# Expert tiles of a cross-attention and mixture-of-experts kernel: gathered rows turned by a transposing DMA instead of by TensorE

## What is computed

```python
x = x + xattn(layernorm(x), ctx)        # x: (4, 1024, 1024), ctx: (4, 1024, 512)
x = x + ffn(layernorm(x))               # 4096 tokens in all
# xattn: q, k = ctx @ Wq.T + bq, ctx @ Wk.T + bk ; attention = softmax(q @ k.T)
#        returns einsum('bln,bmn->blm', layernorm(x), attention)
# ffn, a mixture of 32 experts, 4 of them for each token (H = 1024, I = 512):
logits = x @ gate_w.T + gate_b
top, idx = top_k(logits, 4); weight = softmax(top)
gate = min(xt @ w_gate[e] + b_gate[e], 7); up = clip(xt @ w_up[e] + b_up[e], -7, 7)
act = (up + 1) * gate * sigmoid(1.702 * gate)
y += weight * (act @ w_down[e] + b_down[e])
```

## Time and profile before

| | us |
|---|---|
| median of 3 runs (lowest, highest) | 3435.58 (3431.8, 3443.01) |
| span of the profiled execution | 3448.7 |
| PE busy | 3170.0 (92%) |
| DVE busy | 1738.2 (50%) |
| ACT busy | 1266.2 (37%) |
| POOL busy | 582.6 (17%) |

### The profile page before, as it was taken

How to read it: one execution, slowest core, us unless ns; L and a number is a source line. 1 busy time by engine, 2 the same in 40 slices (tenths; PEclk the granted TensorE clock), 3 DMA queues, 4 the chain that set the end, 5 groups by cost and what they waited for, 6 DMA issues and landing times.

```text
span 3448.7 us, 46558 instructions
## 1 busy us (share of the span) xinstructions
PE 3170.0 (92%) x15456; PEld 1607.2 (47%) x15457; DVE 1738.2 (50%) x2850; ACT 1266.2 (37%) x1299; POOL 582.6 (17%) x502
## 2 busy tenths in 40 slices
PE   6899899987999999999999999999999999999997
PEld 3455555553444444444444444444444444444443
DVE  4576677673444444545544544454444444454432
ACT  4444444333332433334333434343333433332321
POOL 0033323331111111111111111111111111111111
PEclk8899999988999999999999999999999999999999
DMA  3223222354543554645545546564555445454422
GB/s 142 79 105 117 100 94 104 121 168 153 141 140 98 146 140 140 195 136 169 158 134 141 180 132 180 160 182 123 139 175 161 139 141 146 136 164 126 110 61 55
DMA packets 210440, 468.05 MB, mean 136 GB/s; under 512 B 57761, under 2 KB 57761, under 8 KB 210114
## 3 DMA queue, kind: packets, MB, share of 16 engines
q1 hardware_dynamic: 164514, 314.84, 26.5%
q0 software_dynamic: 45856, 152.33, 19.8%
HBM read 354.64 MB, written 112.46 MB: 135 GB/s over the span
## 4 chain that ended last, share of the span: by engine, by line
PE 28%; DMA 27%; issue 11%; DVE 5%; ACT 5%; POOLq 1%; POOL 0%; ACTq 0%; SPq 0%
DMA xg<-xn_tab,idxg 26%; PE psY L1179 22%; DVE y L1104 5%; PE psX L1163 5%; ACT y L1054 5%; PE psG L1157 1%; POOLq L1029 1%; PE psU L1157 0%; POOL acc L1017 0%; DMA acc<-y,idxs 0%; ACTq L1053 0%; POOLq L1033 0%; POOLq L52 0%; ACT xT L1043 0%; DMA idxg<-slots 0%
## 5 line engine op out<-in xcount | busy, mean ns | idle before, releaser
L1179 PE MATMUL psY<-W,aT 128*128 128x512 f16 x3456 | 794.7, 388 | 1.3 <-ACT aT L1047 1.3
L1157 PE MATMUL psG<-W,xT 128*128 128x512 f16 x3456 | 771.7, 380 | 2.8 <-ACT xT L1043 2.8
L1157 PE MATMUL psU<-W,xT 128*128 128x512 f16 x3456 | 769.4, 379 | 0.0
L1017 POOL DMA_INDIRECT acc<-y,idxs x144 | 226.7, 1575 | 2216.0 <-DVE y L1104 2137.3
L1157 PEld LDWEIGHTS psG<-W,xT 128*128 128x128 f16 x3456 | 338.6, 98 | 412.4 <-issue 5.1
L1179 PEld LDWEIGHTS psY<-W,aT 128*128 128x128 f16 x3456 | 345.2, 100 | 396.2 <-issue 33.4
L1157 PEld LDWEIGHTS psU<-W,xT 128*128 128x128 f16 x3456 | 338.2, 98 | 375.6
L1104 DVE SCALAR_TENSOR_TENSOR y<-bias,idxs,y 128x1024 f32<-128x1024 f32 x144 | 185.0, 1285 | 534.2 <-ACT y L1054 534.2
L123 DVE SCALAR_TENSOR_TENSOR W<-stage,W 128x2048 f16<-128x2048 f32 x192 | 437.6, 2279 | 0.0
L1043 ACT ACTIVATE xT<-psX 128x1024 f32<-128x1024 f32 x145 | 148.5, 1024 | 603.6 <-PE psX L1163 603.6
L118 ACT ACTIVATE W<-stage 128x2048 f16<-128x2048 f32 x192 | 365.1, 1902 | 6.8 <-issue 6.6
(11 more groups left out here) (135 smaller groups left out, 2315.4 us busy)
## 6 DMA issues: line engine op xcount, KB each, us to landing
stage<-in_L_ffn_w_gate SPq DMA_DIRECT2D x64, 1024.0 KB, 6.6
stage<-in_L_ffn_w_up SPq DMA_DIRECT2D x64, 1024.0 KB, 6.1
stage<-in_L_ffn_w_down SPq DMA_DIRECT2D x64, 1024.0 KB, 5.0
stage<-in_x SPq DMA_DIRECT2D x32, 512.0 KB, 4.7
xr<-in_x SPq DMA_DIRECT2D x32, 512.0 KB, 4.2
acc<-xr SPq DMA_DIRECT2D x32, 512.0 KB, 2.7
xn_tab<-x2h SPq DMA_DIRECT2D x32, 512.0 KB, 3.0
bias<-in_L_ffn_b_down SPq DMA_DIRECT2D x32, 512.0 KB, 10.2
```

Of the source, the lines that this page charges most:

```text
L1017: pool.indirect_dma_start(out=acc[:, :], out_offset=bass.IndirectOffsetOnAxis(idxs[:, 0:1].bitcast(U32), 0), in_=y[:], in_offset=None, com ...
L1157: op = pe.matmul(ps[:], xT[:, k, :, a], weights(par, c, offset + k * I, I), start=k == 0 and n == 0, stop=k == KH - 1 and n == 2)
L1179: op = pe.matmul(psY[:, h * HALF:(h + 1) * HALF], aT[:, k, :, a], weights(par, c, 2 * KH * I + k * H + h * HALF, HALF), start=k == 0 and n ...
```

## The change

PE's eight transposes of the gathered rows and the PSUM tile `psX` are gone. ACT issues a transposing DMA, SBUF to SBUF, from `xg` into a new buffer `xT_next`, and later copies `xT_next` into `xT`. The high and low parts of a row of the table now lie in two halves, not in pairs, because the DMA turns 2-byte elements. The rows of tile i+2 are turned in step i (before: those of tile i+1). POOL gathers tile j+4 ahead of scatter j (before: tile j+2 ahead of scatter j).

```diff
-        x2h = sb("x2h", [P, 2, H, 2], F16)
+        x2h = sb("x2h", [P, 2, 2, H], F16)
...
         def _(sp):
             load_slots(sp, idxg, 0, s_idxg)
             load_bias(sp, 0, 0)
-            sp.wait_ge(s_xg, 16)
-            load_slots(sp, idxg, 1, s_idxg)
+            for i in range(2):
+                sp.wait_ge(s_xg, 16 * i + 16)
+                load_slots(sp, idxg, i + 1, s_idxg)
             def step(i, e, j, more, prev_guard):
+                sp.wait_ge(s_xg, 16 * i + 48)
+                load_slots(sp, idxg, i + 3, s_idxg)
                 def prev():
                     alone(sp, s_added, i, s_past)
                     load_slots(sp, idxs, i - 1, s_idxs)
                 guarded(sp, prev_guard, prev)
-                sp.wait_ge(s_xg, 16 * i + 32)
-                load_slots(sp, idxg, i + 2, s_idxg)
...
         def _(pool):
             gather(0)
-            pool.wait_ge(s_X, 1)
-            gather(1)
-            pool.wait_ge(s_X, 2)
-            gather(2)
+            for i in range(1, 5):
+                pool.wait_ge(s_xtr, 16 * i)
+                gather(i)
             scatter(0)
-            with pool.Fori(2, tt + 1) as i:
-                pool.wait_ge(s_X, i + 1)
-                gather(i + 1)
-                pool.wait_ge(s_scat, 16 * i - 16)
-                pool.sem_inc(s_added, 1)
-                scatter(i - 1)
+            with pool.Fori(1, before_last) as j:
+                pool.wait_ge(s_xtr, 16 * j + 64)
+                gather(j + 4)
+                pool.wait_ge(s_scat, 16 * j)
+                pool.sem_inc(s_added, 1)
+                scatter(j)
+            for j in (before_last, last):
+                pool.wait_ge(s_scat, 16 * j)
+                pool.sem_inc(s_added, 1)
+                scatter(j)
...
         def _(act):
-            def evac_x(i):
-                act.wait_ge(s_X, i + 1)
-                act.activation(xT[:]...bitcast(F32), psX[:], ACT.Copy).then_inc(s_xTev, 1)
+            def transpose_rows(i):
+                alone(act, s_xg, 16 * i + 16, s_past)
+                act.dma_start_transpose(out=xT_next[:, :, :], in_=xg[:, :]).then_inc(s_xtr, 16)
+            def take_rows(i):
+                act.wait_ge(s_xtr, 16 * i + 16)
+                act.activation(xT[:]...bitcast(F32), xT_next[:]...bitcast(F32), ACT.Copy).then_inc(s_xTev, 1)
...
             def step(i, e, par, t0, j, more, prev_guard):      # ACT, after the second cut
-                evac_x(i + 1)
+                alone(act, s_U, i + 1, s_past)
+                take_rows(i + 1)
+                alone(act, s_xTev, i + 2, s_past)
+                transpose_rows(i + 2)
                 act.wait_ge(s_act, i + 1)
                 act.activation(ahl[:, :, HI], av[:], ACT.Copy, scale=S_ACT).then_inc(s_ahi, 1)
                 guarded(act, prev_guard, lambda: weigh_y(i - 1))
...
         def _(pe):
-                        op = pe.matmul(ps[:], xT[:, k, :, a], weights(par, c, offset + k * I, I),
+                        op = pe.matmul(ps[:], xT[:, a * KH + k, :], weights(par, c, offset + k * I, I),
...
-            def transpose_rows():
-                for n in range(KH):
-                    op = pe.transpose(psX[:, n * P:(n + 1) * P], xg_w[:, n * P:(n + 1) * P], ident[:])
-                op.then_inc(s_X, 1)
...
                 rows_times(psU, par, KH * I, s_U)
-                pe.wait_ge(s_xg, 16 * i + 32)
-                transpose_rows()
                 guarded(pe, prev_guard, lambda: down(i - 1, 1 - par if first else par))
```

More of the change, by code:

```diff
@@ L91, in xattn_moe_kernel @@
     xn_rows = xn_tab.rearrange("(n p) h -> n p h", p=P)
-    slots = nc.dram_tensor("slots", (SLOTS + 2 * P, 4), I32, kind="Internal").ap()
+    slots = nc.dram_tensor("slots", (SLOTS + 3 * P, 4), I32, kind="Internal").ap()
     with ExitStack() as whole:
@@ L366, in _ @@
                              padding).then_inc(s_padout, 16)
-            sp.dma_start(slots[SLOTS:SLOTS + 2 * P, :].rearrange("(o r) c -> o r c", o=1),
-                         padding[0:1, 0:2 * P, :]).then_inc(s_padout, 16)
+            sp.dma_start(slots[SLOTS:SLOTS + 3 * P, :].rearrange("(o r) c -> o r c", o=1),
+                         padding[0:1, 0:3 * P, :]).then_inc(s_padout, 16)
             zero = x2T[:, :, :].rearrange("p k q -> p (k q)")
@@ L409, in step @@
                     sp.dma_start(xn_rows[bass.ds(n, 1)].rearrange("o p h -> (o p) h"),
-                                 x2h[:, s % 2].rearrange("p h a -> p (h a)")).then_inc(s_xnout[s % 2], 16)
+                                 x2h[:, s % 2].rearrange("p a h -> p (a h)")).then_inc(s_xnout[s % 2], 16)
                     if s < NT - 2 or b1 is not None:
@@ L533, in step @@
                     act.wait_ge(s_xs2, tile(bt, n + 1))
-                    act.activation(x2h[:, n % 2, :, HI], xs2[:], ACT.Copy, scale=S_ROWS).then_inc(s_hi2, 1)
+                    act.activation(x2h[:, n % 2, HI, :], xs2[:], ACT.Copy, scale=S_ROWS).then_inc(s_hi2, 1)
                 if b1 is not None:
@@ L785, in step @@
                     dve.wait_ge(s_hi2, tile(bt, n + 1))
-                    dve.scalar_tensor_tensor(out=x2h[:, n % 2, :, LO], in0=xs2[:], scalar=S_ROWS, in1=x2h[:, n % 2, :, HI],
+                    dve.scalar_tensor_tensor(out=x2h[:, n % 2, LO, :], in0=xs2[:], scalar=S_ROWS, in1=x2h[:, n % 2, HI, :],
                                              op0=ALU.mult, op1=ALU.subtract).then_inc(s_lo2, 1)
@@ L866, in _ @@
             dve.wait_ge(s_tail, 3)
+            for back in range(1, 3):
+                link(z, dve.tensor_scalar(tile_start[0:1, E + back:E + back + 1], psE[0:1, E - 1:E], -float(back), None, ALU.add))
             dve.tensor_copy(tile_start[0:1, 1:E + 1], psE[0:1, 0:E]).then_inc(s_tailv, 1)
@@ L906, in experts @@
         xg = sb("xg", [P, 2 * H], F16)
-        xT = sb("xT", [P, KH, P, 2], F16)
+        xT = sb("xT", [P, 2 * KH, P], F16)
+        xT_next = sb("xT_next", [P, 2 * KH, P], F16)
         gt = sb("gt", [P, I], F32)
@@ L914, in experts @@
         y = sb("y", [P, H], F32)
-        xg_w = xg[:, :].bitcast(F32)
         ahl_w = ahl[:, :, :].rearrange("p i a -> p (i a)").bitcast(F32)
@@ L918, in experts @@
         psU = psum("psU", [P, HALF], F32)
-        psX = psum("psX", [P, KH * P], F32)
         psA = psum("psA", [P, KI * P], F32)
@@ L931, in experts @@
         s_U = sem("up_done")
-        s_X = sem("x_transposed")
+        s_xtr = sem("x_transposed")
         s_A = sem("act_transposed")
@@ L951, in start_of, with from_the_end @@
             return eng.value_load(tile_start[0:1, at(nc, e, E)], min_val=0, max_val=MAXT - 4)
+        def from_the_end(eng, back):
+            return eng.value_load(tile_start[0:1, E + back:E + back + 1], min_val=0, max_val=MAXT - 5)
         def load_bias(sp, e, par):
@@ L1005, in _ @@
             load_slots(sp, idxs, tt - 1, s_idxs)
-            alone(sp, s_idxg, 16 * tt + 32, s_past)
+            alone(sp, s_idxg, 16 * tt + 48, s_past)
         @block.gpsimd
@@ L1022, in _ @@
             tt = start_of(pool, E)
+            last, before_last = from_the_end(pool, 1), from_the_end(pool, 2)
             gather(0)
-            pool.wait_ge(s_X, 1)
-            gather(1)
-            pool.wait_ge(s_X, 2)
-            gather(2)
+            for i in range(1, 5):
+                pool.wait_ge(s_xtr, 16 * i)
+                gather(i)
             scatter(0)
-            with pool.Fori(2, tt + 1) as i:
-                pool.wait_ge(s_X, i + 1)
-                gather(i + 1)
-                pool.wait_ge(s_scat, 16 * i - 16)
+            with pool.Fori(1, before_last) as j:
+                pool.wait_ge(s_xtr, 16 * j + 64)
+                gather(j + 4)
+                pool.wait_ge(s_scat, 16 * j)
                 pool.sem_inc(s_added, 1)
-                scatter(i - 1)
+                scatter(j)
[3 more added lines that the diff above has]
+                scatter(j)
             alone(pool, s_xg, 16 * tt + 32, s_past)
@@ L1040, in _ @@
         def _(act):
-            def evac_x(i):
-                act.wait_ge(s_X, i + 1)
-                act.activation(xT[:].rearrange("p k q a -> p (k q a)").bitcast(F32), psX[:], ACT.Copy).then_inc(s_xTev, 1)
+            def transpose_rows(i):
[3 more added lines that the diff above has]
+                act.wait_ge(s_xtr, 16 * i + 16)
+                act.activation(xT[:].rearrange("p k q -> p (k q)").bitcast(F32),
+                               xT_next[:].rearrange("p k q -> p (k q)").bitcast(F32), ACT.Copy).then_inc(s_xTev, 1)
             def evac_a(i):
@@ L1056, in _ @@
             act.sem_inc(s_y0, 1)
-            evac_x(0)
+            transpose_rows(0)
+            take_rows(0)
+            act.wait_ge(s_xTev, 1)
+            transpose_rows(1)
             def step(i, e, par, t0, j, more, prev_guard):
@@ L1097, in _ @@
             weigh_y(tt - 1)
+            alone(act, s_xtr, 16 * tt + 32, s_past)
         @block.vector
```

2 lines of the change are left out of this document (removed).

## The result

The changed kernel takes 3581 us (median of 4 runs, 3576 to 3583), the kernel before 3438 (median of 4): the ratio is 1.041, 95% interval 1.0385 to 1.0433. Slower by 143 us, where 3145 (3095 to 3500) was forecast.

What follows compares the result with a forecast made beforehand. PE was taken as nearly the bound, waiting for the gather; the period falls from 18.22 to 16.2 us over 144 tiles: 3448.7 - 291 - 5 + 2 = 3155 profiled, forecast 3145 us, range 3095 to 3500.

Steps and rivals of the forecast that it cites:

- PE's period without psX: PE's work per tile in the expert stage, without transposes or a wait between up and down product: 15.95, called 16.0 us.
- X: Time of the transposing DMA from issue to landing, 512 KB each way, ACT sequencer time included; taken as 5.0 us.
- 11.2 + X: Mean period in us of the ring over idxs, cuts and table loads included; 16.2 at X = 5.0, break-even at 7.0.
- rival 4: The turn goes as 16 blocks of 128x128 one behind the other: period 36.8 us, time 6110 us; chance 0.10.
- The ring: Per-tile loop of copy into xT, turn, gather issue, idxs, y, sigmoid, aT, second cut; 11.7 + X with cuts, 9.8 + X without.
- landing 1.6: Time in us for SP's load of idxs to land after issue, part of the 3.9 us from gather to idxs.
- PE can absorb a slip of 4.2 us, so the mean decides.: Copy into xT comes after the up product, needed after the down product; so the mean ring length sets the period.
- DMA share 14.1 of 16.2, full but not over: All engines' DMA time per tile: 9.1 us before plus at most 5 for the turn, within a 16.2 us period.
- Rival 3: The same ring decides against the change, X over 7.0, each microsecond above costing 144 us; 3570 at X = 8; chance 0.19.
- rival 1: PE's floor, X up to 4.8: 320 us go, 3113 us; near end of the forecast, which had chance 0.55 with it.
- Small parts: Dense x2h writes in the first stage gain 5 us; first tile's turn costs 3 more, last scatter 1 less.
- 8.4 + X: Length in us of the gather and turn ring through buffer xg; below PE's 16.0 up to X = 7.6.

Runs made afterwards that it cites:

- added_ahead: Changed kernel with POOL raising s_added before its wait for the turn, not behind it and the gather; 3193 us, 0.926 of the kernel before.
- turn_twice: Changed kernel with every turn issued twice, the first into a buffer nobody reads, POOL and ACT waiting for both; 3941 us, 1.143 of the kernel before.
- added_mid: Changed kernel with s_added raised behind the wait for the turn but ahead of the gather; 3371 us, 0.976 of the kernel before.
- no_bias_reload: Changed kernel without the bias loads of experts 1 to 31, so its output differs; 3459 us, 1.004 of the kernel before.
- pe_gather_ahead: Kernel before, PE still turning rows, with POOL gathering tile j+3 ahead of scatter j and SP loading idxg ahead of idxs; 3283 us, ratio 0.950.
- early_turn_twice: added_ahead with every turn issued twice; 3426 us, 0.995 of the kernel before.
- bias_ahead: Changed kernel with the next expert's three bias loads issued before the same step's three weight loads; 3577 us, 1.035 of the kernel before.

## Why the prediction was wrong

- **PE's period without psX.** Right: 16.0 was worked out, 15.98 is the median in added_ahead, and 16.85 with PE's turn and no wait.
- **X, the price of the turn.** The one unknown was taken at 5.0 and is 4.4 as a median: on the right side. By the prediction's own sum that should have given PE's floor, 3113. But the prediction says that the mean decides, and the mean of X is 5.9; by 11.2 + X that is a period of 17.1, still faster than before. The Trainium skill's 261 GB/s ("DMA: Bandwidth & Descriptors", Latency and other measured facts) would make the transfer an estimated 2.0 us of the 4.4. The trace has no row that splits them; the packets of a turn took 2.9 us of all 16 engines, an estimated 180 GB/s and so less than that figure. The Trainium skill's block figure ("VectorE: DVE Perf Modes", The three transpose paths) does not add up block by block here: sixteen blocks land in 4.4 us, where sixteen times 1309 ns is 20.9, so rival 4 is out.
- **The ring.** Right in its order, and that ACT's wait for `idxs` would be its mark. Its lengths were not: SP issues `idxs` 1.7 us behind the turn's landing (1.02 and 0.70), where 2.3 was given as the sign. added_ahead shows it by taking it away, turn_twice by stretching it: 2.6 us of turn, 2.5 us a tile.
- **The step that failed is "landing 1.6" in the ring.** I took the landing of `idxs` from a moment when nothing was in front of it. In the new order it is issued 0.7 us behind a gather of 512 KB and lands in 3.9. That is 2.3 us a tile, 144 x 2.28 = 328 us, and added_mid shows the cause: issued just ahead of the gather, it takes 1.7. The prediction said itself that the gather stands in front of `s_added`, and costed only its issue. The time from gather to `idxs` was taken 1.3 too long, since the scatter's wait is over by then; the net is +1.0. added_mid also shows that the late turns alone do not make the kernel slower: with the short landing, and 0.9 us of the gather's issue out of the ring besides, the mean period is 17.71 with the late turns still there, under the 18.22 of before. The two parts of that move were not taken apart.
- **"PE can absorb a slip of 4.2 us, so the mean decides."** The mean did decide, but X went into it without a tail; this is the second term that was mis-sized. The turn shares the engines with a burst of 4 MB, and the mean from its issue to the gather is 1.5 above the median (6.93 against 5.46) and 1.6 above the 5.3 of the sum. Between `y` and the sigmoid the mean is 0.7 above the median (4.20 against 3.53), about half of it waits for biases and half pairs of table loads on ACT, of which the prediction counted 16 single ones; against the sum's 3.8 that is 0.4. no_bias_reload takes 1 MB of the 4 away and gets 122 us back. "DMA share 14.1 of 16.2, full but not over" looked at the mean of a load that comes in bursts, and took 5 us of all engines for a turn that used 2.9. So the break-even was not X = 7.0. The period is 0.9 above that of before at X = 4.4, and turn_twice showed a microsecond for a microsecond, so I estimate it near a median X of 3.5, below the turn's 4.4 us.
- **Rival 3 was the outcome** (the same ring decides against the change), at a price of X that rival 1 was meant for.
- **Small parts.** ACT's write of `x2h` fell from 1356 ns to 1056, DVE's from 1387 to 1225. The first gather is issued at 774.8 to 781.6 us in the ten kernels with the new layout and at 787.4 to 791.3 in the three with the old: nearer 10 us than the 5 that was taken. The weight loads were rightly put at nothing: ACT's cut waits 5.5 us for them in all. Two slips changed nothing: X = 6 gives 3286 us by the prediction's sum and not 3270, and the gather's 6.1 us in "8.4 + X" held only behind the scatter (last section).
- **Not weighed at all:** how much of the expected gain needs no turn by DMA. pe_gather_ahead gets 5.0% from the order on POOL and SP alone; the DMA turn adds 2.7% to that (3193 against 3283) if its ring is open, and takes 9% away (3581 against 3283) if it is not.

## What to carry to other kernels

When a signal is moved behind a longer wait, list every semaphore that the waiting engine raises after that wait, and close each ring that goes through them; a signal that doesn't need the wait goes ahead of it. Price a small load by what is issued just in front of it in the new order, not by its best landing, and give a step that shares the DMA engines with bursts a mean and not a median. Before paying for a new mechanism, try the reordering that comes with it alone.

## What was not expected of the hardware

- The issue of a transposing DMA is not short: it holds ACT's queue for 2.4 us as a median and up to 7.9, where SP's plain issues in the same kernel, 2 to 1024 KB, have medians of 0.34 to 0.60. With the engines at a share of 0.87 and two turns a tile ACT's next instruction waited behind it for 1087 us in all (early_turn_twice).
- 146 turns made 303,680 packets, 2080 each of some 252 bytes (76.56 MB over them), and took 11.9% of 16 engines over 3580 us, 2.9 us of all engines for each turn.
- A 2 KB load behind a 512 KB gather, issued 0.7 us later, landed in 3.9 us; 0.17 us ahead of it, in 1.7.
- The gather of 512 KB lands in 6.1 us in the kernel before, where it is issued 1.9 us behind the scatter, and in 4.4 in bias_ahead, where the last scatter was issued 9.9 us earlier.
